# Stage boundaries by halves in a four-block perceiver kernel: the stream added in PSUM, the layernorm shared by two engines

## The reference, cut to what matters

```python
xn = layernorm(x)              # (x - mean) / sqrt(var + eps), 128 features
x = x + layer(xn)              # layer: l0x l0a l0f | l1x l1a l1f | l2x l2a l2f | l3x l3a l3f
# l0a: layer(xn) = (layernorm(o) * gamma + beta) * silu(gate) @ Wo        (a norm inside)
# l2x: y = xn + attn(xn); z = ln(y) * g1 + be1; a = y + ffn(z)
#      x = x + ln(a) * g2 + be2                                          (two norms inside)
# l2a: z = ln(attn(xn) @ Wo + bo + xn); x = x + ln((z @ W1 + b1) @ W2 + b2 + z)
# l2f: four rounds cur = cur + mixture(cur), from cur = xn
# l3a: z = ln(xn) * g + b; x = x + attn(z) @ Wproj + bp + z
```

## Time and profile before

| what | value |
|---|---|
| three runs | 1411.76, 1412.07, 1527.96 us; median 1412.07 us |
| profiled execution, its own time | 1411.98 us |
| its span in the trace | 1410.2 us |
| mean granted PE clock | 0.859 of full speed |
| PE busy | 1123.4 us, 80% of the span |
| DVE busy | 777.9 us, 55% |
| ACT busy | 567.7 us, 40% |
| POOL busy | 311.3 us, 22% |

### The profile page before, as it was taken

How to read it: one execution, slowest core, us unless ns; L and a number is a source line. 1 busy time by engine, 2 the same in 40 slices (tenths; PEclk the granted TensorE clock), 3 DMA queues, 4 the chain that set the end, 5 groups by cost and what they waited for, 6 DMA issues and landing times.

```text
span 1410.2 us, 26546 instructions
## 1 busy us (share of the span) xinstructions
PE 1123.4 (80%) x8781; PEld 835.6 (59%) x8781; DVE 777.9 (55%) x2135; ACT 567.7 (40%) x1162; POOL 311.3 (22%) x498
## 2 busy tenths in 40 slices
PE   5758998999995368999965143799999979998537
PEld 2326665788774346788843142576677758887434
DVE  2364444555554944677857394533333357776692
ACT  2233223434332133677742212434344437776122
POOL 1000001121120104555510010304040315554010
PEclk8577998999998568999977555899999989999657
DMA  8410120222220003455500301011111111111000
GB/s 279 137 60 1 45 70 11 55 60 48 56 60 1 2 1 98 110 147 146 154 1 0 45 2 37 23 56 45 56 45 45 56 31 32 30 30 35 1 1 15
DMA packets 70989, 75.03 MB, mean 53 GB/s; under 512 B 6273, under 2 KB 63697, under 8 KB 70537
## 3 DMA queue, kind: packets, MB, share of 16 engines
q1 hardware_dynamic: 67864, 66.18, 17.3%
q0 software_dynamic: 1152, 6.97, 1.4%
q10 hardware_dynamic: 1904, 0.98, 0.5%
HBM read 71.49 MB, written 0.52 MB: 51 GB/s over the span
## 4 chain that ended last, share of the span: by engine, by line
PE 72%; DVE 17%; ACT 4%; DMA 3%; issue 2%; ACTq 1%; POOL 1%; SPq 0%; DVEq 0%; POOLq 0%
PE PS L460 13%; PE PS L472 12%; PE PS L817 9%; PE PS L670 4%; DVE AR L1319 4%; PE PS L827 4%; PE PS L634 4%; PE PS L439 3%; PE PS L431 3%; PE PS L621 2%; PE PS L463 2%; PE PS L677 2%; PE PS L800 2%; DVE ST L1323 2%; PE PS L847 2%
## 5 line engine op out<-in xcount | busy, mean ns | idle before, releaser
L472 PEld LDWEIGHTS PS<-WB,AR 128*128 128x128 f32 x1568 | 190.7, 193 | 43.9 <-issue 40.1
L472 PE MATMUL PS<-WB,AR 128*128 128x128 f32 x1568 | 190.8, 276 | 0.0
L945 ACT ACTIVATE AR<-PS,WB 128x512 f32<-128x512 f32 x160 | 109.9, 687 | 159.5 <-PE PS L460 153.4
L1431 DVE SCALAR_TENSOR_TENSOR ACC<-PS,SM,ACC 128x128 f32<-128x128 f32 x256 | 72.2, 345 | 127.4 <-PE PS L472 126.0
L817 PE MATMUL PS<-AR 128*128 128x257 f32 x512 | 138.6, 393 | 2.1 <-POOL AR L2099 1.9
L460 PE MATMUL PS<-ZT,WB 128*128 128x512 f32 x208 | 103.8, 624 | 3.9 <-ACT ZT L964 3.5
L817 PEld LDWEIGHTS PS<-AR 128*128 128x128 f32 x512 | 87.1, 190 | 21.9 <-issue 7.7
L1319 DVE TENSOR_TENSOR AR<-PS,AR 128x512 f32<-128x512 f32 (+2 forms) x69 | 48.4, 701 | 91.3 <-issue 39.4
L460 PE MATMUL PS<-XNT,WB 128*128 128x512 f32 x168 | 89.9, 643 | 5.5 <-ACT AR L945 3.9
L945 ACT ACTIVATE AR<-PS 128x512 f32<-128x512 f32 (+2 forms) x81 | 43.7, 540 | 114.0 <-PE PS L463 68.1
L945 ACT ACTIVATE AR<-PS,SM 128x257 f32<-128x257 f32 x136 | 64.6, 475 | 37.2 <-DVE SM L1503 27.6
(11 more groups left out here) (225 smaller groups left out, 2212.7 us busy)
## 6 DMA issues: line engine op xcount, KB each, us to landing
WB<-in_units SPq DMA_DIRECT2D x49, 385.0 KB, 3.1
CTX<-in_fside SPq DMA_DIRECT2D x32, 514.0 KB, 4.0
CTX<-in_ctxT SPq DMA_DIRECT2D x96, 130.0 KB, 2.1
CTX<-in_ctxT SPq DMA_DIRECT2D x8, 520.0 KB, 4.1
CTX<-in_ctxN SPq DMA_DIRECT2D x16, 258.0 KB
CTX<-in_ctxN SPq DMA_DIRECT2D x32, 129.0 KB, 2.3
AR<-in_ctxN SPq DMA_DIRECT2D x32, 64.5 KB, 2.9
AR<-in_l1x_w POOLq DMA_DIRECT2D x1, 2048.0 KB, 8.5
```

Of the source, the lines that this page charges most:

```text
L472: m = pe.matmul(PS[:, 4 + hh, 128 * t:128 * t + 128], f_h[hh][:, c, 128 * t:128 * t + 128], WB[:, q, 2 * UNIT + 128 * c:2 * UNIT + 128 * c ...
L945: return act.activation(o, i, fn, **k)
L1431: ins = dve.scalar_tensor_tensor(out=a, in0=y, scalar=f_w[:, 4 * hh + t, bass.ds(e, 1)], in1=a, op0=ALU.mult, op1=ALU.add)
```

## The change

Half one of each norm is done by ACT, as an activation with scale 1/std and bias -mean/std, half two by DVE. Each half has its own square root. Where a projection ends a layer, PE first multiplies the stream by the identity into banks 6 and 7 (`carry`) and the projection accumulates onto it; statistics and normalisation read PSUM, and the sum is copied back to `X` after the transposes. ACT copies bank 0 of the transposes, DVE bank 1, and PE waits for each half by itself. The affine of l2x's first inner norm goes into those copies; l0a's rows are multiplied by the gate on POOL beforehand; three additions to the stream and one bias addition move to POOL. Table loads for the next function come after ACT's copies.

```diff
@@ PE
+            def half_taken(hh):
+                name = ("turned_a", "turned_d")[hh]
+                pe.wait_ge(sig[name], seen.up(name))
+            def x_written(hh, k):
+                pe.wait_ge(sig[("x_half_a", "x_half_d")[hh]], k)
+            def carry(src):
                 for hh in range(2):
+                    pe.matmul(bank(6 + hh), ident, flat(src)[:, 512 * hh:512 * hh + 512], start=True, stop=False,
+                              skip_group_check=True)
+            def wide(k, weight, src, fresh=False):
+                for hh in range(2):
+                    if fresh:
+                        half_taken(hh)
...
-                                  src[:, P * t:P * t + P], weight, start=True, stop=True)
+                                  src[:, P * t:P * t + P], weight, start=False, stop=True, skip_group_check=True)
...
+            carry(X)
+            wide(4, w("l0x_v"), l0_ut, True).then_inc(sig["lin_ready"], 1)
             pe.wait_ge(sig["lin_taken"], seen.up("lin_taken"))
             project(l0_ct, w("l0x_o"))
...
+            x_written(0, 2)
             for t in range(NT):
+                if t % 4 == 0:
+                    half_taken(t // 4)
                 m = pe.matmul(PS[:, 6, 8 * t:8 * t + 8], XNT[:, P * t:P * t + P], w("l0f_gate"),
...
+            pe.matmul(bank(6), ident, flat(X)[:, 0:512], start=True, stop=False, skip_group_check=True)
             pe.wait_ge(sig["yo_taken"], seen.up("yo_taken"))
-            for t in range(NT):
-                m = pe.transpose(PS[:, 6 + t // 4, 128 * (t % 4):128 * (t % 4) + 128], OT[:, P * t:P * t + P], ident)
...
+            project(OT, ident, second_half)
...
                 core()
+                if bias:
+                    pe.wait_ge(sig["bias_ready"], bias)
+                carry(X)
                 project(OT, w(o))
...
+            pe.wait_ge(sig["acc_ready"], 2)
+            carry(ACC)
...
-                turn(XN) if r == 0 else turn(ACC, None)
+                turn(XN) if r == 0 else turn(ACC, "down_used")
@@ ACT
+            def norm(src, dst, eps=eps_col):
                 prepare(ACT.Sqrt)
+                def root(hh):
+                    act.wait_ge(sig["var_ready"], seen.up("var_ready"))
+                    f(SD[:, 0, 4 * hh:4 * hh + 4], MV[:, 4 * hh:4 * hh + 4, 1], ACT.Sqrt, bias=eps)\
...
+                def tile(t):
+                    f(dst[:, t, :], src(t), bias=SD[:, 2, t:t + 1], scale=SD[:, 1, t:t + 1])\
+                        .then_inc(sig["norm_act"], 1)
...
+                root(0)
+                act.wait_ge(sig["shift_ready"], seen.up("shift_ready"))
+                for t in range(3):
+                    tile(t)
+                root(1)
+                tile(3)
+            def turned(dst, then=None, carried=False, **affine):
+                act.wait_ge(sig["turned"], seen.up("turned"))
+                f(dst[:, 0:512], PS[:, 0, :], **affine).then_inc(sig["turned_a"], 1)
...
+                if carried:
+                    act.copy(flat(X)[:, 0:512], PS[:, 6, :]).then_inc(sig["x_half_a"], 1)
...
                 if then:
                     prepare(then)
@@ DVE
+            def moments(hh):
+                dve.wait_ge(sig["dve_ran"], seen.up("dve_ran", 0))
+                for t in range(4 * hh, 4 * hh + 4):
+                    dve.bn_aggr(MV[:, t, :], ST[:, t, :]).then_inc(sig[name], 1)
...
+            def first_shift():
                 dve.wait_ge(sig["std_ready"], seen.up("std_ready"))
+                dve.reciprocal(SD[:, 1, 0:4], SD[:, 0, 0:4]).then_inc(sig["dve_ran"], 1)
+                dve.scalar_tensor_tensor(out=SD[:, 2, 0:4], in0=MV[:, 0:4, 0], scalar=-1.0, in1=SD[:, 1, 0:4],
...
+            def layernorm(src, dst, carried=False):
+                if carried:
                     dve.wait_ge(sig["proj_ready"], seen.up("proj_ready"))
+                stats(src, range(4))
+                moments(0)
+                if carried:
+                    dve.wait_ge(sig["proj_ready"], seen.up("proj_ready"))
+                stats(src, (4, 5))
+                first_shift()
+                stats(src, (6, 7))
+                moments(1)
+                second_tiles(src, dst)       # reciprocal, four tensor_scalar
...
+            def turned(dst, carried=False, g=None, b=None):    # copies bank 1; with carried, bank 7 to X
...
                 def last_unit(e):
+                    add(e, 0)
+                    stats(tile_of(into), range(4))
+                    moments(0)
+                    add(e, 1)
+                    first_shift()
+                    stats(tile_of(into), range(4, NT))
+                    moments(1)
...
-            affine(Z[:, :, :], "l2x_g1", "l2x_be1").then_inc(sig["stream_ready"], 1)
+            layernorm(carried_tile, Z, True)
+            turned(ZT[:, :], g=z_scale, b=z_shift)
...
-            tt(flat(X), flat(X), flat(ACC), ALU.add).then_inc(sig["resid_done"], 1)
-            layernorm(X, XN, LN_EPS)
+            second_tiles(tile_of(X), XN)         # the last round adds into X itself
@@ POOL
+            for dst, name in ((ACC, "l0a_gamma"), (ACCB, "l0a_beta")):
+                pool.tensor_tensor(dst[:, :, :], ar(5120, 1024).rearrange("p (t n) -> p t n", t=NT), rows_t(name),
+                                   ALU.mult).then_inc(sig["gate_scaled"], 1)
...
+            normed(10)
+            pool.tensor_tensor(Z[:, 0:4, :], Z[:, 0:4, :], rows_t("l2x_g2", 4), ALU.mult).then_inc(sig["z_scaled"], 1)
...
+                    pool.tensor_tensor(X[:, :, :], X[:, :, :], ACC[:, :, :], ALU.add).then_inc(sig["x_summed"], 1)
```

More of the change, by code:

```diff
@@ L788, in _, with cross @@
             m.then_inc(sig["gate_mm"], 1)
-            ff("l1f", XNT)
-            def cross(kname, vname, biased):
+            ff("l1f", XNT, second=True)
+            def cross(kname, vname, biased, src, bias=None):
                 sel = w("head_mask")[:, 0:32]
@@ L927, in _ @@
             turn(XN)
-            wide(2, w("l3x_q"), XNT).then_inc(sig["xq_mm"], 1)
-            cross("l3x_k", "l3x_v", False)
+            wide(2, w("l3x_q"), XNT, True).then_inc(sig["xq_mm"], 1)
+            cross("l3x_k", "l3x_v", False, X, 9)
             project(OT, w("l3x_o"))
-            self_attention("l3a_q", "l3a_k", "l3a_v", "l3a_o")
+            self_attention("l3a_q", "l3a_k", "l3a_v", "l3a_o", 5, 10)
             turn(XN)
-            wide(6, w("l3f_u1"), XNT).then_inc(sig["lin_ready"], 1)
-            pe.wait_ge(sig["lin_taken"], seen.up("lin_taken"))
-            ff("l3f", f_pt)
-            turn(ACC, None)
-            project(ZT, w("l3f_v2"))
+            for hh in range(2):
+                half_taken(hh)
+                pe.matmul(bank(2 + hh), w("l3f_u1"), XNT[:, 512 * hh:512 * hh + 512], start=True, stop=True)\
+                    .then_inc(sig["lin_ready"], 1)
+            hidden(0)
+            hidden(1)
+            ff("l3f", f_pt, second=True, close=False)
+            pe.wait_ge(sig["bias_ready"], 11)
+            x_written(0, 6)
+            x_written(1, 6)
+            carry(X)
+            turn(ACC, "down_used")
+            project(ZT, w("l3f_v2"), half_taken)
         @block.scalar
@@ L1013, in _ @@
             act.wait_ge(sig["w_first"], 16)
-            norm_std(ACT.Exp)
-            turned(XNT[:, :])
+            norm(tile_of(X), XN)
+            turned(XNT[:, :], ACT.Exp)
             act.wait_ge(sig["lin_ready"], seen.up("lin_ready"))
@@ L1245, in cross @@
                 seen.up("xu_ready")
-            norm_std(ACT.Exp)
-            turned(XNT[:, :])
+            norm(tile_of(X), XN)
+            turned(XNT[:, :], ACT.Exp)
             cross(None)
-            norm_std(LAYERS_FF["l2x"][1])
-            turned(ZT[:, :])
+            norm(carried_tile, Z)
+            turned(ZT[:, :], LAYERS_FF["l2x"][1], scale=z_scale, bias=z_shift)
             ff("l2x")
-            norm_std()
-            norm_std(ACT.Exp)
-            turned(XNT[:, :])
+            norm(tile_of(ACC), Z)
+            norm(tile_of(X), XN)
+            turned(XNT[:, :], ACT.Exp)
             act.wait_ge(sig["lin_ready"], seen.up("lin_ready"))
```

466 lines of the change are left out of this document (294 added, 172 removed).

## The result

The changed kernel takes 1366.56 us (median of 4 runs, 1366.13 to 1370.04) against 1412.06 us; the ratio is 0.968, with a 95% interval of 0.966 to 0.970. That is 45.5 us, where 31.6 were forecast. Its profiled execution, the slowest of the four, took 1370.04 us with a span of 1368.2, so its trace holds 42.0 of them, and the mean granted clock rose from 0.859 to 0.884. Three slow executions are left out of all comparisons: two of the kernel before (1527.96 us, and 1816.5 beside e9 to e12) and one of e5 (2894.69).

The account below looks back on a forecast made before the run. PE bounds the kernel, and the change can pay only at boundaries where PE waits. Carried boundaries 13.2 plus others 14.7, less 1.3 for tiles, plus clock 5, give 31.6 us off 1411.98: 1380 us, range 1366 to 1394.

Parts of the forecast that it names:

- tiles at 0.40: Normalised tiles taken at 0.40 us instead of 0.37, on fourteen norms: 1.3 us off the gain.
- The unit: One carried layer boundary, DVE's start to next product: 5.95 us against 8.16, 2.2 gained, 1.7 where the projection runs half-clocked.
- half one's lead is unused: At every boundary ACT's half-two tiles set the start; listed as a rival, already counted in the unit, no chance given.
- The clock: PE holds full clock at three of six boundaries with a fast projection: 5 us gained, bounds 0 and 14.
- The carries: Nine added pairs of identity products, each 2.00 us at full clock, 3.79 at half; partly hidden where PE stood idle.
- inside l0a: The norm inside l0a, its gamma, beta and gate operations shortened, products starting behind the first half: 2.8 us gained.
- at l3f: Exposed carry costs 2.8 us, boundary gains 2.2, and the split input product overlaps copies: net 0.2 us lost.
- start with the gate at 87 and end by 92, before DVE wants them at 101: Inside l0a, POOL's two moved operations of 2.35 us finish before DVE needs their results.
- Tables: Rival, slower: table loads of 1.28 us between ACT's roots and tiles on 18 norms, 1426 to 1449 us; chance 0.04.
- Carries paid at the half-clock price: Rival: all carries run at half clock and no boundary holds its clock, 1392 us; chance 0.26.
- Longer ACT: Rival: ACT's serial tiles take 0.46 us or more, 0.5 on each of fourteen norms, 1387 us; chance 0.12.
- The clock holds nearly everywhere: Rival: PE keeps full clock at nearly all boundaries, 9 us more gain, 1371 us; chance 0.15.

Follow-up runs that it names:

- e9: The changed kernel, unchanged, run and traced a second time: 1368.96 us.
- e12: The changed kernel with two added identity products ahead of the transposes of each normalised input, where PE stands idle: 1357.45 us.
- e5: The changed kernel with every normalisation in one piece on DVE, keeping the carry and the waits by halves: 1372.80 us.
- e11: The kernel before, with PE waiting for the second half of the transposed input only ahead of what reads it, except at l0a: 1386.00 us.
- e1: The changed kernel without carries: DVE adds the projection's banks to the stream again at all ten places: 1369.06 us.
- e3: The changed kernel with DVE normalising all eight tiles and ACT taking only the two roots: 1368.36 us.
- e7: The changed kernel with PE waiting for both halves of the transposed input ahead of its first product: 1399.96 us.
- e10: The changed kernel without carries, with whole normalisations on DVE and PE waiting for both halves of the transposed input: 1407.93 us.
- e4: The kernel before, with two identity products, their result overwritten, added where the changed kernel has its carries: 1419.63 us.
- e6: The changed kernel without carries and with every normalisation in one piece on DVE, waits by halves kept: 1371.85 us.

## Why the prediction was right, and where it was not

The sign and the range held, but the result lies 0.6 us inside the range's lower edge, and that it lies inside is partly luck: the term that outgrew its forecast did so by a way that the prediction didn't name. The trace gained 42.0 us where 31.6 were forecast. In the sum, the 1.3 us taken off for tiles at 0.40 are counted twice, since the unit was worked out with 0.40 already.

**The unit** held in size: 5.77 at layer 1 and 5.48 inside l2x for the 5.95 forecast. ACT's three tiles took 1.15 us (0.38 each, forecast 0.40), its second root needed no table load, and DVE's four took 1.37, starting 3.78 us after the first statistics. What the unit did not show is what its parts are worth. Taken singly at layer 1, waiting by halves gives 0.94 of the 2.4 (e11). The carry gives 1.05 (e1), and where it is exposed it takes about as much back over the trace. The order by halves and ScalarE's tiles give 0.9 (e5), ScalarE's own part of that being 0.2 (e3). The prediction held that "half one's lead is unused", because no product starts before the eighth transpose, and it had the product right behind that transpose, with both copies off the path. That is so, and the unit holds the 0.94 in it. But it put the gain down to carry, tiles and order, and didn't see that PE, which no longer stops between transposes and products, is back at full clock sooner. With the waits by halves undone, all the rest together is worth 12 to 14 us (e7); with carry, tiles and order undone as well, 4 (e10).

**The clock** is the term that was mis-sized: 5 us of bounds 0 to 14, where 26 us less busy time at half clock are 13 (and 18 by e9's trace). The prediction looked for boundaries held by a fast projection and by carries. Here is the busy time at half clock by kind of work, with each stretch of one microsecond weighed as above. "Added" are carries, or the products that e4 and e12 add.

| kernel | added | projections | transposes | all other work |
|---|---|---|---|---|
| before | | 22 | 31 | 171 |
| e4 before, with the products added | 16 | 11 | 31 | 175 |
| e10 | | 22 | 30 | 173 |
| e7 both halves waited for | 18 | 9 | 27 | 159 |
| e11 before, halves waited for singly | | 19 | 29 | 151 |
| e6 no carry, norm in one piece | | 21 | 28 | 151 |
| e1 no carry | | 20 | 33 | 149 |
| after | 18 | 8 | 22 | 149 |
| e9 after, again | 14 | 8 | 20 | 146 |
| e12 after, with idle PE filled | 18 | 11 | 9 | 132 |

The mechanism that the prediction named is there: with the carries, the projections and the transposes have 23 to 26 us less at half clock (after and e9 against e1). But the carries spend 14 to 18 themselves, so that 5 to 12 are left, 2 to 6 us of time. What the prediction didn't have is the last column. All other work has 171 to 175 in the kernel before, e4 and e10, which wait for both halves, and 146 to 151 in e11, e6, e1, after and e9, which wait by halves. e7, with both waits and the rest of the change, has 159. e11 shows that the waits alone bring it, and e10 that it goes with them. The runs don't show why a wait of 0.7 us less does this at one boundary and not at another: in after and in e11 l3x's first product still starts at half clock. The sum over the whole trace is what they show.

**The carries** before l0x_v, l1f and l3f took 3.62, 3.65 and 3.78 us. As forecast, the first takes over the half clock of l0x_v's product (2.35 us where it was 3.78). Behind the one before l1f the projection ran at full clock (1.95 us); before l3f it took 3.04, mostly at half clock. l1f came at -1.2 for -1.0.

**Stage by stage** the trace gained (forecast in brackets): to l0a 1.2 (1.1 with the first norm), inside l0a 1.7 (2.8), l0f -0.2 (-0.7), l1x 1.9 (1.45), l1a 1.4 (0.8), l1f -1.2 (-1.0), l2x 4.1 (1.45), inside l2x 8.1 (6.8), l2a 2.5 (1.05), its second norm 4.1 (1.4), l2f 3.7 (2.65), the rounds to the third 6.4 (4.05), l3x 4.1 (3.3), l3a 2.9 (2.65), l3f -2.8 (-0.2), the rest 4.1 (0.3). The second trace (e9) has 2.8 to l0a, 2.9 for the second norm of l2a, 4.0 for l3a, -1.3 for l3f and 1.4 for the rest, with the other stages within 1 us. So single stages are known to 1 to 3 us only, and the list doesn't say where the excess over the forecast comes from.

**Two terms fell short in both traces, in part for a cause that the prediction had not looked at**, inside l0a and at l3f. Both have work moved to POOL. That its operations "start with the gate at 87 and end by 92, before DVE wants them at 101" speaks of their results only. The timeline of before has DVE's operation at the gate, and its first mask product in layer 3, alone:

```profile
87.41 1.22 DVE L1319 TENSOR_TENSOR AR<-AR 128x1024 f32<-128x1024 f32 x1
...
1328.38 2.29 DVE L1319 TENSOR_TENSOR AR<-AR,W 128x2048 f32<-128x2048 f32 x1
```

In the timeline after, the same DVE operations (two mask products in one row) stand beside POOL's:

```profile
86.46 2.43 POOL L2242 TENSOR_TENSOR ACC<-AR,RB 128x1024 f32<-128x1024 f32 x1 [12.92 <-ACT AR L1035]
88.85 3.37 POOL L2242 TENSOR_TENSOR ACCB<-AR,RB 128x1024 f32<-128x1024 f32 x1
...
86.65 3.31 DVE L1436 TENSOR_TENSOR AR<-AR 128x1024 f32<-128x1024 f32 x1
...
1287.31 4.39 POOL L2398 TENSOR_TENSOR X<-X,Z 128x1024 f32<-128x1024 f32 x1 [11.43 <-DVE Z L1436]
...
1287.20 6.65 DVE L1436 TENSOR_TENSOR AR<-AR,W 128x2048 f32<-128x2048 f32 x2
```

3.31 for 1.22, and 6.65 for two of 2.29; the trace of e9 has the same two lengths. Not all of these 4.1 us lie on the path. In l0a DVE had stood 1.26 us for a product of PE a little behind this operation, and that wait is gone, so that some 0.9 us reach the chain, about the shortfall (1.1, and 0.7 in e9). At l3f DVE's operations follow each other without a pause, and the carry starts 2.1 us later within its stage than the projection did before (0.7 in e9, whose first products there ran 1.0 shorter). The rest of the shortfall is no more than the carry's excess, 3.78 us for the 2.8 forecast. POOL's operations waited too, 3.37 for 2.43 and 4.39 for the 2.35 of the earlier trace rows. In the trace neither shares its time: DVE's operation ends 1.1 us, nearly its own length, after POOL's first. At l3f DVE's first mask product, begun 0.1 us ahead of POOL's operation, takes its 2.29 us; POOL's ends 2.2 us behind it, at 1291.70, and DVE's second ends 2.15 behind that. The Trainium skill (SBUF — State Buffer, section Who interferes with whom) says that a VectorE instruction with two SBUF inputs and a GpSimd instruction that reads SBUF exclude each other for a whole instruction. These rows agree. No run left POOL's work out, so that the 3 us would come back is worked out from the rows, not shown by a run.

**The rivals.** Tables: no load stands between the roots. Carries paid at the half-clock price: true of five of the nine in the first trace (3.43 to 3.78 us; the others took 1.88 to 2.40), but not of the sum. Longer ACT: no, 0.38 a tile. The clock holds nearly everywhere (1371): nearest to the result in its number only, since 197 of 223 us at half clock are left. The mean clock of 0.884 is inside what was said.

## What to carry to other kernels

Before rebuilding the arithmetic of a stage boundary, look at what the first product really waits for: here splitting one wait in two, with no operation changed, gave 26 us in the kernel before, where the whole change gave 45 (e11). Judge an edit by two sums over the trace, the gaps at boundaries and the busy time at half clock, of which half counts; split the second by kind of work, and take two traces, since one kernel's differ by 10 us. Work added to keep the clock up pays where PE is still at full clock when it runs (e12), and not where it runs at half clock itself (e4). When work moves to POOL, look also at what DVE does at that moment, not only at when the result is needed.

## What the runs showed of the hardware

- Two products of 128x512 put into an idle time of some 3 us, 1.98 us long at full clock, went with l3x's first product at 2.4 GHz: 2.07 us, for 3.78 and 2.92 without them. Over the trace 2 us of the added work ran at half clock, and the transposes had 9 us at half clock for 20. The same products directly ahead of projections of the kernel before spent 16 us at half clock themselves and saved 11 in the projections.
- ACT normalises three tiles of 128x128 from PSUM in 1.15 us with pointer scale and bias (0.38 each; a single one takes 0.46) and goes from square root to this and back without a table load.
- DVE and POOL, each with a tensor_tensor that reads SBUF: on DVE 1.22 becomes 3.31 us, and 2.29 twice becomes 6.65; on POOL 2.35 becomes 4.39.
